# Forming, splitting and transposing the expert gates earlier, on GpSimd from the third batch on

## The reference

```python
x = x + xattn(layernorm(x), ctx, ctx)   # 8 heads of 16; the softmax runs over the HEADS (axis=1)
x = x + ffn(layernorm(x))

# ffn: 8 experts, hidden size 256, the best 2 of 8 chosen per token
logits   = x @ Wr + br
sel      = one_hot(top_k(logits, 2)).sum(-2) > 0
gates    = softmax(where(sel, logits, -max))
h        = relu(einsum('btd,edh->bteh', x, W1) + b1)
out      = einsum('bte,bteh,ehd->btd', gates, h, W2) + einsum('bte,ed->btd', gates, b2)
```

## Time and profile before

| | us |
|---|---|
| median of 3 runs | 207.93 (207.81 to 209.05) |
| the profiled execution | 208.05 |
| its span in the trace | 206.2 |
| TensorE busy | 193.4 (94%) |
| VectorE busy | 171.9 (83%) |
| ScalarE busy | 133.8 (65%) |
| GpSimd busy | 120.1 (58%) |

### The profile page before, as it was taken

The page is one execution under the profiler, slowest core; times in us unless marked ns, Lnnn a source line. Parts: engine busy times, 40 slices in busy tenths (PEclk is TensorE's granted clock), DMA queues, the critical chain, the costliest instruction groups (busy, mean ns, idle before and its releaser), DMA issues.

```text
span 206.2 us, 4730 instructions
## 1 busy us (share of the span) xinstructions
PE 193.4 (94%) x1600; PEld 170.7 (83%) x1600; DVE 171.9 (83%) x460; ACT 133.8 (65%) x318; POOL 120.1 (58%) x154
## 2 busy tenths in 40 slices
PE   6999997989998999999999999998999899979995
PEld 6449965976987799978899789978997799779994
DVE  5799986999999989998898989897999979356543
ACT  6257768957776568766777776776667665444541
POOL 6123959998699729376944967196729773220010
PEclk9999999999999999999999999999999999999999
DMA  6968789345024505041242324140000000000000
GB/s 167 275 214 208 174 268 259 106 135 153 5 102 127 156 26 174 10 150 33 102 102 78 103 103 105 60 119 3 0 24 4 2 0 14 15 3 0 27 2 29
DMA packets 20360, 18.74 MB, mean 91 GB/s; under 512 B 1776, under 2 KB 18800, under 8 KB 20336
## 3 DMA queue, kind: packets, MB, share of 16 engines
q1 hardware_dynamic: 19904, 18.04, 30.6%
q10 hardware_dynamic: 432, 0.39, 0.6%
HBM read 11.88 MB, written 6.55 MB: 89 GB/s over the span
## 4 chain that ended last, share of the span: by engine, by line
PE 66%; DVE 19%; issue 7%; POOL 6%; ACT 1%; DVEq 0%; POOLq 0%; ACTq 0%
PE y_ps L449 20%; PE h_ps L434 12%; PE misc_ps L390 6%; PE score_ps L371 6%; DVE acc L1026 4%; PE h_ps L379 4%; DVE attn L943 4%; PE score_ps L359 3%; PE score_ps L348 2%; DVE shift_m L935 2%; PE score_ps L292 2%; PE score_ps L434 2%; DVE ln_stats L895 1%; POOL gatesD L1244 1%; PE misc_ps L399 1%
## 5 line engine op out<-in xcount | busy, mean ns | idle before, releaser
L703 ACT ACTIVATE hT<-h_ps,b_sb 128x256 f32<-128x256 f32 x118 | 49.4, 470 | 31.1 <-PE h_ps L434 31.1
L449 PE MATMUL y_ps<-w_sb,hT 128*128 128x128 f32 x508 | 67.7, 276 | 0.0
L449 PEld LDWEIGHTS y_ps<-w_sb,hT 128*128 128x128 f32 x508 | 62.8, 192 | 1.8 <-issue 0.7
L1212 POOL TENSOR_TENSOR half_sum<-e_sb 128x512 f32<-128x512 f32 x28 | 37.6, 1344 | 21.0 <-ACT e_sb L675 21.0
L943 DVE TENSOR_TENSOR attn<-e_sb,e_rcp 128x1024 f32<-128x1024 f32 x32 | 48.2, 1511 | 0.6 <-ACT e_rcp L686 0.6
L935 DVE TENSOR_REDUCE shift_m<-score_ps 128x128 fp32r<-128x1024 f32 x32 | 38.5, 1211 | 0.3 <-PE score_ps L348 0.3
L675 ACT ACTIVATE e_sb<-score_ps 128x1024 f32<-128x1024 f32 x32 | 32.6, 1022 | 7.9 <-PE score_ps L371 5.9
L434 PE MATMUL h_ps<-x1T_hi,w_lo 128*128 128x256 f32 x118 | 37.4, 320 | 0.2
L1026 DVE SCALAR_TENSOR_TENSOR acc<-y_ps,gates,acc 128x128 f32<-128x128 f32 x96 | 28.9, 342 | 7.7 <-PE y_ps L449 6.1
L434 PE MATMUL h_ps<-x1T_hi,w_hi 128*128 128x256 f32 x118 | 32.9, 281 | 0.0
L434 PE MATMUL h_ps<-x1T_lo,w_hi 128*128 128x256 f32 x118 | 31.9, 281 | 0.0
(11 more groups left out here) (122 smaller groups left out, 276.9 us busy)
## 6 DMA issues: line engine op xcount, KB each, us to landing
k_scratch<-k_parts SPq DMA_DIRECT2D x14, 256.0 KB, 2.6
k_stack<-k_scratch SPq DMA_DIRECT2D x14, 256.0 KB, 4.0
q_stack<-q_scratch SPq DMA_DIRECT2D x28, 128.0 KB, 2.7
q_scratch<-q_parts SPq DMA_DIRECT2D x7, 256.0 KB, 2.1
w_sb<-in_w SPq DMA_DIRECT2D x1, 1024.0 KB, 6.3
out_y<-y_out SPq DMA_DIRECT2D x7, 128.0 KB, 1.8
x_all<-in_x SPq DMA_DIRECT2D x1, 768.0 KB, 6.4
ctxT<-in_ctx_t SPq DMA_DIRECT2D x1, 640.0 KB, 7.2
```

Source lines behind the costliest of these rows:

```text
L449: mm = nc.tensor.matmul(product(j, t), hT[:, j % 2, c, t * P:(t + 1) * P], w2_sb[:, e * HC + c, :], start=(c == 0), stop=(c == HC - 1))
L703: op = nc.scalar.activation(hT[:, j % 2, c, :], hidden(j)[:, c * S:(c + 1) * S], ACT.Relu, bias=b1_sb[:, e * HC + c:e * HC + c + 1])
L1212: nc.gpsimd.tensor_tensor(half_sum[:], e[:, 0:HQ // 2], e[:, HQ // 2:HQ], ALU.add).then_inc(sum_step, 1)
```

## The change

On VectorE, `make_gates` ends after `gate_of` for batches 2 to 7, and the transposition stands ahead of the residual instead of behind the layer norm. On GpSimd a new `place_gates` forms `gated_onehot` and `gates` for these batches; it and `split_gates` stand first in the period, and `block_gates` stands ahead of `ln2_end`. The counts of the semaphore `router_step` follow (`router_steps`). The written beginning, with batches 0 and 1, keeps its order.

```diff
--- before.py
+++ after.py
@@ -160,6 +160,7 @@
         logits_done, logits_step, logits_made, router_step, gap_made, gap_exp_made, gates_made = (
             sem("logits_done"), sem("logits_step"), sem("logits_made"), sem("router_step"), sem("gap_made"), sem("gap_exp_made"),
             sem("gates_made"))
+        gates_placed = sem("gates_placed")
         gates_zeroed, gate_step, gatesT_made, gates_blocked, b2_done, b2_added = (
             sem("gates_zeroed"), sem("gate_step"), sem("gatesT_made"), sem("gates_blocked"), sem("b2_done"), sem("b2_added"))
         h_done, relu_made, y_done, gated = sem("h_done"), sem("relu_made"), sem("y_done"), sem("gated")
@@ -168,7 +169,7 @@
             [sem("last_done0"), sem("last_done1")], [sem("last_gated0"), sem("last_gated1")],
             [sem("last_stored0"), sem("last_stored1")])
         LAST = E * B - 1
-        ROUTER_STEPS = 7
+        POOL_GATES = 2
 
         def wait(eng, semaphore, n):
             if n > 0:
@@ -176,6 +177,9 @@
 
         def there(b):
             return 0 <= b < B
+
+        def router_steps(b):
+            return 7 * min(b, POOL_GATES) + 6 * max(b - POOL_GATES, 0)
 
         def summed_on_pe(n):
             return n < PE_SUMS
@@ -956,7 +960,7 @@
             def choose_experts(b):
                 if b == 0:
                     dve.wait_ge(pool_made, 1)
-                at = ROUTER_STEPS * b
+                at = router_steps(b)
                 dve.wait_ge(logits_made, b + 1)
                 for t in range(TT):
                     op = nc.vector.max(top8[:, t, :], logits[:, t, :])
@@ -972,13 +976,15 @@
                                         ALU.is_equal).then_inc(router_step, 1)
 
             def make_gates(b):
-                at = ROUTER_STEPS * b + 3
+                at = router_steps(b) + 3
                 dve.wait_ge(gap_exp_made, b + 1)
                 nc.vector.tensor_scalar(gap_exp1[:], gap_exp[:], 1.0, None, ALU.add).then_inc(router_step, 1)
                 dve.wait_ge(router_step, at + 1)
                 nc.vector.reciprocal(gate_of[:, 0, :], gap_exp1[:]).then_inc(router_step, 1)
                 dve.wait_ge(router_step, at + 2)
                 nc.vector.tensor_tensor(gate_of[:, 1, :], gate_of[:, 0, :], gap_exp[:], ALU.mult).then_inc(router_step, 1)
+                if b >= POOL_GATES:
+                    return
                 dve.wait_ge(router_step, at + 3)
                 nc.vector.tensor_tensor(gated_onehot[:], onehot[:], gate_of[:].unsqueeze(3).to_broadcast([P, 2, TT, E]),
                                         ALU.mult).then_inc(router_step, 1)
@@ -1068,14 +1074,14 @@
                     normalize(now, 0)
                 if there(g):
                     add_expert(g, 1)
+                if there(g):
+                    transpose_gates(g)
                 if there(f):
                     add_residual(f)
                 if there(g):
                     add_expert(g, 2)
                 if there(f):
                     ln2(f)
-                if there(g):
-                    transpose_gates(g)
                 if kv < B:
                     k_lo(kv)
                 if there(now):
@@ -1225,6 +1231,15 @@
                 pool.wait_ge(ln2_neg_made, b + 1)
                 nc.gpsimd.tensor_tensor(ln2_off[:], ln2_neg[:], ln2_rstd[:], ALU.mult).then_inc(ln2_off_made, 1)
 
+            def place_gates(b):
+                pool.wait_ge(router_step, router_steps(b + 1))
+                pool.wait_ge(gated, E * (b - 1))
+                nc.gpsimd.tensor_tensor(gated_onehot[:], onehot[:], gate_of[:].unsqueeze(3).to_broadcast([P, 2, TT, E]),
+                                        ALU.mult).then_inc(gates_placed, 1)
+                pool.wait_ge(gates_placed, b - POOL_GATES + 1)
+                nc.gpsimd.tensor_tensor(gates[:, b % 2], gated_onehot[:, 0], gated_onehot[:, 1],
+                                        ALU.add).then_inc(gates_made, 1)
+
             def split_gates(b):
                 pool.wait_ge(gates_made, b + 1)
                 if b == 0:
@@ -1261,16 +1276,17 @@
 
             def period(i):
                 now, f, g = i - 2, i - 3, i - 4
+                if there(g):
+                    place_gates(g)
+                    split_gates(g)
                 if there(now):
                     head_sum(now, 0)
-                if there(g):
-                    split_gates(g)
                 if there(now):
                     head_sum(now, 1)
+                if there(g):
+                    block_gates(g)
                 if there(f):
                     ln2_end(f)
-                if there(g):
-                    block_gates(g)
                 if there(now):
                     head_sum(now, 2)
                 if there(now):
```

## The result

The changed kernel takes **203.11 us** (median of 4 runs, 202.99 to 203.2); the kernel before, beside it, 207.87 (4 runs). The ratio is 0.9746, 95% interval 0.9723 to 0.977. 203.2 was forecast. The profiled execution took 203.2 us, its span is 201.4.

The account below looks back on a forecast made before the run. TensorE, 94% busy, bounds the kernel, its idle time waiting mainly for the spread `gatesD`. From the profiled 208.05 us, -4.40 - 0.65 + 0.30 = -4.75 us gives 203.3, or 203.2 us beside the median; range 202.3 to 205.9.

Parts of the forecast that it names:

- Step 1: Transposition and spread move ahead: TensorE's waits at L409 go in batches 2 to 6, 4.40 us, counting 0.16 more each.
- "Just enough" for L303: TensorE's transposition of `xn`: the `b2` addition can be there at 122.27, L303 could start at 122.34, 0.57 us earlier.
- VectorE paces: Rival, 10%: VectorE does not bring the `b2` addition forward because an `attn` runs late; 1.5 us lost, 204.7 us.
- L303 with no new wait: Sign of being right: TensorE's transposition of `xn` gets no new wait; idle time there put down to `add_b2` means wrong.
- Step 2: VectorE loses two instructions per period; in batch 2's period `head_max` starts earlier and the wait before L371 goes: 0.65 us.
- Step 3: GpSimd's four gate instructions ahead of its first sum take 1.14 us, making it 0.55 us later in batch 3's period.
- the 0.3 us given back: Batch 2's period, where the sum is late by 1.1 us, returns 0.3 us of its second gain; bounds 0 and 0.65.
- the slack: How late the first `e_sum` may be before `headsT` delays TensorE's L399: 1.0 us, of which 0.55 is used.
- late sums: Rival, 17%: a gate instruction falls behind an `attn`, the sum is 1.6 us late, four periods lose 2.4 us: 205.6 us.
- slower: Rival, 6%: a gate instruction and `half_sum` queue behind VectorE, L399 waits 1.9 us in four periods: 210.8 us.
- long gate instruction: Sign of being wrong: gate instructions of a microsecond on GpSimd, where the four together were to take 1.1 to 1.2 us.
- Step 4: VectorE's expert 0 now waits for GpSimd's `gates`, some 0.2 us late in batches 6 and 7; cost nothing.

Follow-up runs that it names:

- moves_only: The kernel before with only the transposition (VectorE) and the spread (GpSimd) moved early, gates still formed on VectorE: 203.87 us, ratio 0.9786.
- spread_only: The kernel before with only GpSimd's spread moved ahead of the layer norm's power: 204.75 us, ratio 0.9831.
- transpose_only: The kernel before with only VectorE's transposition moved ahead of the residual: 208.39 us, ratio 1.0005.
- gates_only: The changed kernel with both moves undone, gates still formed and split on GpSimd ahead of its sums: 207.59 us, ratio 0.9982.

## Why the prediction was right

**Step 1, the moves: right, size too.** All five waits went, and the three distances of batches 3, 5 and 6 hit the forecast within 0.04 us. `moves_only`, which has this step alone, gained 0.55, 0.61, 1.06, 1.06 and 1.17 us in batches 2 to 6, where 0.57, 0.57, 1.00, 1.07 and 1.19 were forecast. That supports counting 0.16 us more per wait than the row lists. `spread_only` and `transpose_only` add what the prediction did not say: without the spread's move the transposition's is worth nothing.

**"Just enough" for L303 was not enough once.** Batch 4 lacks 0.29 us, and the sign that the prediction asked for, L303 with no new wait, failed there: the addition could start 0.70 us after the `b2` matmuls by the forecast, and started after 0.97. The rival *VectorE paces* named the place and the releaser, but neither its cause (no late `attn`) nor its size (1.5 us). The runs show a pause of 0.36 us at one place in VectorE's list, which no row of the kernel before shows.

**Step 2, the collision: right.** 0.65 us forecast in batch 2; `moves_only` keeps the collision and gains 0.55 us there, the change, without it, 1.30.

**Step 3: the prices right, the 0.3 us given back wrong.** `gated_onehot` took 0.24 us and `gates` 0.22 (0.25 and 0.22 forecast). Batch 2 gained 1.30 where 1.22 was the most expected, so its sum was not too late, but it was close: `headsT` ended 0.20 us ahead of the projection, and 0.15 is where TensorE waits. The forecast took 0.45 us as left of the slack; 0.62 is measured in batch 3. The rivals *late sums* and *slower* failed in the same step: they passed every microsecond ahead of the sum on to the logarithm. The `attn` and the sums here do not run side by side, which costs one of them some 1 us in any case (2.36 us instead of 1.22, or 2.28 instead of 1.27), and what GpSimd does meanwhile without reading is not lost: a fill of 0.95 us made the sum 0.25 us later. The Trainium skill ("SBUF — State Buffer", Who interferes with whom) says that a VectorE instruction with two SBUF inputs contends with GpSimd's reads and not with one that only writes; the trace agrees, 1.22 us beside the fill against 2.36 beside the `half_sum`. The chance of *late sums* also rests on a miscount: not one batch in six but two show a long copy in the kernel before, 1.20 us in batch 2 beside the 1.14 in batch 6. Its long gate instruction, one of the signs of being wrong, did come, once, in the period of batch 6, where VectorE's expert 0 then waits for TensorE and not for the gates (GpSimd of the changed kernel):

```profile
171.22 1.18 POOL L1240 TENSOR_TENSOR gates<-gated_onehot 128x16 f32<-128x16 f32 x1
```

**Step 4: right.** I put the gates 0.2 us late in the last periods. VectorE of the changed kernel, batch 7, and of the kernel before, from its last `gate_of`:

```profile
188.12 0.61 DVE L1032 SCALAR_TENSOR_TENSOR acc<-y_ps,gates,x 128x128 f32<-128x128 f32 x2 [0.75 <-POOL gates L1240]
```

```profile
191.97 0.16 DVE L981 TENSOR_TENSOR gate_of<-gate_of,gap_exp 128x2 f32<-128x2 f32 x1
...
192.70 0.61 DVE L1026 SCALAR_TENSOR_TENSOR acc<-y_ps,gates,x 128x128 f32<-128x128 f32 x2
```

Expert 0 starts 0.75 us after `gate_of` ends, in the kernel before 0.57: 0.18 us late. That period is 0.11 us longer, but not for this: `gates_only` has the same wait of 0.75 us and the distance of the kernel before, 13.79 us, while `moves_only`, without the wait, has 13.88. The 0.1 us comes with the moves; why stays open.

The errors, 0.38 us too little in batch 2 and 0.29 and 0.11 too much in batches 4 and 7, cancel by luck; the sum is better than its terms.

## What to carry to other kernels

Work off the critical path is worth moving when a wait on it ends last: here 0.6 us of work, moved past 0.9 us of other work, gave 3.4 us, as it recurs five times. A delay in front of instructions that already queue behind another engine is not passed on one to one; ask what they would have waited for anyway. And measure small effects from one recurring row to the next, since the start of this program alone varies by more than a microsecond.

## What the hardware showed unexpectedly

- Which of `attn` and a sum goes first changes from period to period (2.36 and 1.27, or 1.22 and 2.28 us); the pair takes 2.4 us either way.
- The pause of 0.36 us follows a place in VectorE's list: 0.83 to 0.84 us there in six kernels, 0.49 with two fills put ahead at the start. What happens at that place stays open. The Trainium skill ("Runtime: NRT & Kernel Launch", Instruction fetch mechanics) says that instructions are loaded in blocks and that crossing a block's end is mostly hidden; that would fit a pause by place, but no run here shows that a load causes it. The traces do have packets of the kind `instruction`. One of 8 KB starts 0.67 to 0.68 us after the paused row's start in all six kernels, though that row stands anywhere from 119.00 to 120.53 us; in the seven in which VectorE waits there without a pause one starts 0.83 to 0.91 us ahead of the same row. So a load shifts with the pause, but comes after it, and no row says whose list it loads.
